# Moving the values of a 64-token window attention behind the scores, two pairs at a time

## The reference, cut to what matters

```python
def _layer(x, wqkv, qs, ksc, wo, lg, lb, w1, b1, w2, b2):
    h = shift_token(x)              # second half of the channels, one token later
    q, k, v = split_heads(h @ wqkv) # 8 heads of 64
    q = l2norm(q) * qs
    k = l2norm(k) * ksc
    q, k = rotary_xpos(q, k)
    # 64-token windows, each sees itself and the window before it:
    sim = einsum('bhwid,bhwjd->bhwij', q * 8, k)  # masked
    attn = softmax(sim)
    o = einsum('bhwij,bhwjd->bhwid', attn, v)
    x = x + o @ wo
    ...                             # token shift, layer norm, gated MLP
```

## Time and profile before

| | |
|---|---|
| median of 3 runs | 2771.79 us |
| the profiled execution | 2765.04 us, its span 2763.1 us |
| PE busy | 2596.0 us, 94% |
| ACT busy | 1839.9 us, 67% |
| DVE busy | 1642.4 us, 59% |
| POOL busy | 1025.6 us, 37% |
| mean granted clock of PE | 0.983 |

### The profile page before, as it was taken

How to read it: one execution, slowest core, us unless ns; L and a number is a source line. 1 busy time by engine, 2 the same in 40 slices (tenths; PEclk the granted TensorE clock), 3 DMA queues, 4 the chain that set the end, 5 groups by cost and what they waited for, 6 DMA issues and landing times.

```text
span 2763.1 us, 61433 instructions
## 1 busy us (share of the span) xinstructions
PE 2596.0 (94%) x23844; PEld 1789.5 (65%) x23844; DVE 1642.4 (59%) x4295; ACT 1839.9 (67%) x4424; POOL 1025.6 (37%) x876
## 2 busy tenths in 40 slices
PE   7999999899999998999999997998998998988998
PEld 4655656449899884788888883554555663553554
DVE  6564747475545548556666666774774236755774
ACT  6676767427676661778787875875785417776775
POOL 2332323213323310545454533552553014542551
PEclk9999999999999998999999999999999999999999
DMA  1010000000000002000000003111210002201210
GB/s 59 1 44 1 13 10 1 4 9 2 2 2 2 2 2 61 21 2 2 2 2 2 2 2 127 47 35 28 54 47 5 25 20 60 49 20 35 50 39 16
DMA packets 35411, 63.13 MB, mean 23 GB/s; under 512 B 11542, under 2 KB 15670, under 8 KB 34102
## 3 DMA queue, kind: packets, MB, share of 16 engines
q1 hardware_dynamic: 35126, 59.21, 7.8%
HBM read 23.62 MB, written 1.15 MB: 9 GB/s over the span
## 4 chain that ended last, share of the span: by engine, by line
PE 76%; DVE 8%; ACT 7%; issue 3%; SPq 3%; POOL 1%; DMA 1%; DVEq 0%; POOLq 0%; ACTq 0%
PE bank L807 65%; PE bank L1036 6%; PE bank L1173 3%; SPq L772 3%; ACT work L1430 1%; ACT work L1323 1%; PE bank L883 1%; DVE work L1619 1%; ACT bank L1299 1%; ACT squared L1301 1%; DMA work<-work 1%; ACT squared L1295 1%; ACT work L1291 1%; POOL work L1993 1%; DVE centered L1550 1%
## 5 line engine op out<-in xcount | busy, mean ns | idle before, releaser
L1749 DVE TENSOR_REDUCE low<-bank 128x1 f32<-128x512 f32 (+22 forms) x512 | 292.9, 573 | 290.6 <-PE bank L807 288.8
L1291 ACT ACTIVATE low<-bank 128x512 f32<-128x512 f32 (+3 forms) x544 | 434.4, 919 | 0.0
L807 PE MATMUL bank<-table_keys,halves 128*128 128x512 f32 (+3 forms) x1536 | 414.9, 378 | 2.6 <-ACT low L1384 2.4
L807 PE MATMUL bank<-work 128*64 128x128 f32 (+6 forms) x4192 | 343.2, 294 | 40.8 <-DVE work L1841 20.4
L807 PEld LDWEIGHTS bank<-work 128*64 128x64 f32 (+4 forms) x4192 | 248.6, 144 | 204.7 <-issue 149.8
L1384 ACT ACTIVATE low<-bank,low 128x512 f32<-128x512 f32 (+23 forms) x384 | 224.9, 586 | 228.4 <-DVE low L1749 223.2
L1944 POOL TENSOR_TENSOR halves<-squared,const 128x512 fp32r<-128x512 f32 x128 | 135.6, 1060 | 502.1 <-PE bank L807 502.1
L1291 ACT ACTIVATE work<-bank 128x512 f32<-128x512 f32 (+4 forms) x389 | 199.8, 539 | 132.9 <-PE bank L807 67.9
L807 PEld LDWEIGHTS bank<-table_keys,halves 128*128 128x128 f32 x1536 | 241.9, 189 | 42.2 <-issue 11.9
L1430 ACT ACTIVATE work<-work 128x192 f32<-128x192 f32 (+1 forms) x512 | 218.7, 431 | 38.5 <-DVE work L1834 38.5
L1993 POOL TENSOR_TENSOR work<-work 128x768 f32<-128x768 f32 x128 | 187.7, 1467 | 136.0 <-DVE work L1845 136.0
(11 more groups left out here) (203 smaller groups left out, 5373.2 us busy)
## 6 DMA issues: line engine op xcount, KB each, us to landing
work<-work SPq DMA_DIRECT2D x512, 64.0 KB, 2.0
slot<-in_wW SPq DMA_DIRECT2D x4, 1605.5 KB, 6.6
slot<-in_wA SPq DMA_DIRECT2D x4, 837.0 KB, 6.1
table_low<-embv_padded SPq DMA_DIRECT2D x2, 1536.0 KB, 6.4
table<-in_dft SPq DMA_DIRECT2D x1, 3072.0 KB, 11.7
slot<-in_wE SPq DMA_DIRECT2D x2, 584.0 KB, 3.8
squared<-in_x SPq DMA_DIRECT2D x4, 256.0 KB, 6.4
shifted<-embv_padded SPq DMA_DIRECT2D x2, 512.0 KB, 8.2
```

The lines of the kernel that those rows point to most:

```text
L807: return pe.matmul(o, l, r, start=start, stop=stop)
L1291: return act.activation(dst, src, ACT.Identity)
L1749: dve.tensor_reduce(out=NBR[:, t.G % 4:t.G % 4 + 1], in_=bank[t.G % 2][:, 0:score_columns(t)], axis=AX.X, op=ALU.max, negate=True).then_in ...
```

## The change

The values step of the loop now does both pairs of one `hp` at once. It stands in every even step from the fifth on, right behind the scores and ahead of the projection, and takes the pairs j - 4 and j - 3; the heads copy follows the exponentials of the same step. `TW` has four buffers. The token shift at the start of a stage goes lane by lane; the clearing of `PW` is moved behind the last lane's shift, and DVE's first reduction of a stage waits for it.

```diff
@@ stage_w, the loop over the steps
                     add("w_scores", c=lane, i=i, hp=hp)
+                if j >= 4 and j % 2 == 0:
+                    lane, i, hp = pairs[j - 4]
+                    held = add("w_values", c=lane, i=i, hp=hp, u=first + j - 4)
                 if r < C * lane_items:
                     rotate(r)
                 if j < len(pairs):
+                    lane, i, hp = pairs[j]
                     add("w_exps", c=lane, i=i, hp=hp)
-                if 2 <= j <= len(pairs) + 1:
-                    lane, i, hp = pairs[j - 2]
-                    if i == 0:
-                        held = add("w_values", c=lane, i=i, hp=hp, u=first + j - 2)
-                    else:
-                        add("w_values_on", c=lane, i=i, hp=hp, u=first + j - 2, tile=held)
-                        add("w_heads", c=lane, hp=hp, tile=held)
+                if j >= 4 and j % 2 == 0:
+                    lane, i, hp = pairs[j - 4]
+                    add("w_heads", c=lane, hp=hp, tile=held)
                 if r < C * lane_items:
                     length(r)
@@ buffers
-        TW = carve(2, 2, T)
+        TW = carve(4, 2, T)
@@ PE
-            def head_values(s, o):
-                pe.wait_ge(sem("w_turned_act"), s.u + 1)
-                pe.wait_ge(sem("w_turned_dve"), s.u + 1)
-                for u in range(2):
-                    i = s.i + u
+            def w_values(s):
+                if s.hp == 0:
+                    pe.wait_ge(sem("w_v_copied"), NT * (s.u // 8 + 1))
+                pe.wait_ge(sem("w_turned_act"), s.u + 2)
+                pe.wait_ge(sem("w_turned_dve"), s.u + 2)
+                o = take(s.k)
+                for i in range(NT):
                     for blk in range(0 if i else 1, 2):
                         for a in range(2):
                             h = 2 * s.hp + a
                             last = mm(o[a * 64:(a + 1) * 64, i * P:(i + 1) * P], VW[:, s.c % 2, i - 1 + blk, h * 64:(h + 1) * 64],
-                                      TW[:, s.u % 2, u, (2 * a + blk) * P:(2 * a + blk + 1) * P],
+                                      TW[:, (s.u + i // 2) % 4, i % 2, (2 * a + blk) * P:(2 * a + blk + 1) * P],
                                       start=(blk == (0 if i else 1)), stop=(blk == 1))
...
+                last.then_inc(tile_full, 1)
@@ ACT, w_heads
-                act.wait_ge(sem("w_valued"), s.n + 1)
-                copy(AW[:, s.hp, :], tile_of(s.tile.k)[:, :]).then_inc(sem("w_heads_copied"), 1)
+                copy(AW[:, s.hp, :], full(s.tile.k)[:, :]).then_inc(sem("w_heads_copied"), 1)
@@ DVE, w_scores
+                if s.c == 0 and s.hp == 0 and s.i == 0:
+                    dve.wait_ge(sem("pad_cleared"), s.n // (DEPTH_W * C * PAIRS * NT // 2) + 1)
@@ POOL, shift
-                if s.c == 0 and s.via == "norm":
-                    for lane in range(C):
-                        source_ready(pool, s, lane)
-                    stage = s.n // (2 * DEPTH_W * C)
-                    pool.memset(PW.rearrange("p a b t -> p (a b) t")[:, :, 0:P], 0.0).then_inc(sem("pad_cleared"), 1)
-                    pool.wait_ge(sem("pad_cleared"), stage + 1)
                 pool.tensor_copy(shifted[0:half, s.c, :], inner[0:half, s.c, :])
                 pool.tensor_copy(shifted[half:P, s.c, 1:T], inner[half:P, s.c, 0:T - 1]).then_inc(sem("shift_done"), 1)
                 pool.wait_ge(sem("shift_done"), s.n + 1)
+                if s.c == C - 1 and s.via == "norm":
+                    stage = s.n // (2 * DEPTH_W * C)
+                    pool.memset(PW.rearrange("p a b t -> p (a b) t")[:, :, 0:P], 0.0).then_inc(sem("pad_cleared"), 1)
+                    pool.wait_ge(sem("pad_cleared"), stage + 1)
```

More of the change, by code:

```diff
@@ L1275, in _ @@
                          w_rotate=w_rotate, w_length=w_length, w_value=w_value, w_scores=w_scores, w_turn=w_turn,
-                         w_values=w_values, w_values_on=w_values_on, w_out=w_out, w_mlp=w_mlp, h_kernels=h_kernels,
+                         w_values=w_values, w_out=w_out, w_mlp=w_mlp, h_kernels=h_kernels,
                          h_project=h_project, h_turn=h_turn, h_forward=h_forward, h_inverse=h_inverse, h_out=h_out)
@@ L1434, in turned_columns @@
                 v, lo = "p (a b t) -> p a b t", 0 if s.i + u else 1
-                return (TW[:, s.n % 2, u].rearrange(v, a=2, b=2)[:, :, lo:2, :], bank_[:, :].rearrange(v, a=2, b=2)[:, :, lo:2, :])
+                return (TW[:, s.n % 4, u].rearrange(v, a=2, b=2)[:, :, lo:2, :], bank_[:, :].rearrange(v, a=2, b=2)[:, :, lo:2, :])
             def w_turn(s):
@@ L1840, in w_turn @@
                 o = full(s.k + 1)
-                dve.tensor_copy(TW[:, s.n % 2, 1], o[:, :]).then_inc(sem("w_turned_dve"), 1)
+                dve.tensor_copy(TW[:, s.n % 4, 1], o[:, :]).then_inc(sem("w_turned_dve"), 1)
             def w_weigh(s):
@@ L1911, in shift @@
                     pool.wait_ge(sem("first_cleared"), 1)
-                if s.c == 0 and s.via == "norm":
-                    for lane in range(C):
-                        source_ready(pool, s, lane)
+                pool.tensor_copy(shifted[0:half, s.c, :], inner[0:half, s.c, :])
+                pool.tensor_copy(shifted[half:P, s.c, 1:T], inner[half:P, s.c, 0:T - 1]).then_inc(sem("shift_done"), 1)
+                pool.wait_ge(sem("shift_done"), s.n + 1)
+                if s.c == C - 1 and s.via == "norm":
                     stage = s.n // (2 * DEPTH_W * C)
@@ L1918, in shift @@
                     pool.wait_ge(sem("pad_cleared"), stage + 1)
-                pool.tensor_copy(shifted[0:half, s.c, :], inner[0:half, s.c, :])
-                pool.tensor_copy(shifted[half:P, s.c, 1:T], inner[half:P, s.c, 0:T - 1]).then_inc(sem("shift_done"), 1)
-                pool.wait_ge(sem("shift_done"), s.n + 1)
             def gate(s):
```

## The result

| | before | after |
|---|---|---|
| median of 4 runs, us | 2773.27 (2771.15 to 2778.8) | 2823.97 (2821.84 to 2826.74) |
| the profiled execution, us | 2765.04, span 2763.1 | 2821.84, span 2819.9 |
| PE busy, us | 2596.0 | 2594.0 |
| ACT busy, us | 1839.9 | 1840.7 |
| mean granted clock of PE | 0.983 | 0.984 |

The changed kernel is slower: ratio 1.0184, 95% interval 1.017 to 1.0197, which is 51 us. 2812 was forecast, with 2783 to 2836 around it. PE and ACT do the same amount of work as before; what is new is waiting.

What follows compares the result with a forecast made beforehand. PE alone was taken to bound the attention loop. Four loops at +12.6 us give +50.4, the shift -10.0, together +40.4 on the median 2771.8: 2812 us, range 2783 to 2836.

Steps and rivals of the forecast that it cites:

- Projection to length 1.81: In each loop step with a projection, nothing lies between it and its length: 1.81 us start to start, range 1.60 to 2.0.
- 28 values in 1.65: Every second step, 28 value matmul records run together behind the scores, taking 1.65 us.
- +1.32: Steps 4 to 23 of a loop: each pair of steps takes 1.32 us more, ten pairs +13.2 a loop.
- ACT on time: In the step with values, ACT's queue takes 4.36 us between squares, PE needs 4.60: ACT is ready 0.2 early.
- Copies' waits, -1.0: First 24 steps of a loop: waits for ACT's copies of turned probabilities shrink, saving 1.0 us, ends 0 and 1.6.
- the -0.3: Steps 2 and 3 of a loop: the values only vanish there, -0.3 us a loop.
- twice 0.4 for the output projection: Output projection waits for the last heads copy: 0.2 to 0.4 us lost, twice a loop, +0.7.
- The last eight steps, 0: Loop steps without a projection: taken as 0 us a loop, between ends -5.0 and +3.8.
- The two halves: Last eight steps: up to 5.0 us of values' waits for DVE's copies won, against doubled values delaying turns, up to 3.8.
- Shift, -10: Start of the two stages: lane-by-lane shift brings ACT's first square 5.0 us earlier, twice, -10.0 us, ends -10 and 0.
- The faster rival: Loop: fewer mode changes and vanished values' waits win, and the length finds its square ready; 2718 us, chance 0.05.
- The rival of the clock: First 24 steps of the loops: PE's short stalls lower its granted clock to 0.96, 21 us more, 2833; chance 0.03.

## Why the prediction was right, point by point

- **Projection to length 1.81:** right. It is 1.81 or 1.82 in steps 4 to 23 of all four loops, taken from the one place in the old trace that had nothing in between the earlier trace rows. The runs with a later length, and with values or a value projection in between, make the idle time go exactly where something lies between.
- **28 values in 1.65:** measured 1.68. Two steps: 10.54 against 9.22, +1.32 as forecast.
- **ACT on time:** right, with 0.49 to spare where 0.2 was reckoned. It becomes the bound only once the wait for the square is removed, which the run with the later length shows.
- **Copies' waits, -1.0:** about -0.8, as what is left over. Ten pairs of steps at 1.32, the -0.3 and twice 0.4 for the output projection (which came as forecast: 0.39 each) make 13.7; measured 12.9.
- **The last eight steps, 0:** this is the term that was mis-sized. It is 2.8 + 0.9 = 3.7 a loop, 15 us in all, at the high end that was named (3.8). The two halves were thought to cancel. The gain did not come, since the wait for the weighing stands right behind those waits for copies and takes their place, as the single values three steps back show. The cost came in full and more: fewer values ahead of the turn uncover POOL's order (add, then weighing), and in three of four loops the wait is followed by a dip of the clock. About half of it, 7 us, goes with single values at the end, and exchanging POOL's add takes back 0.7 to 2.2 a loop by its trace; the two were not run together, so how far they overlap is open. In the old order the same exchange only moves the wait to the next step.
- **Shift, -10:** 4.7 and 5.0 in the trace, 11 us by the run of the shift alone.
- **The sum.** By the runs of single parts the loop costs 60.7 where 50.4 was forecast, and the shift gives 11.0 where 10.0 was. By the trace the loops cost 66.4, and nearly all that is over the forecast is the term of the last eight steps; 12.9 for the first 24 steps stands against 12.6 forecast.

The faster rival had the price of a change between kinds of matmul right. A projection behind split matmuls takes 1.05 before another split group (above, 1748.27 to 1749.32) and 0.96 before a full one (1738.08 to 1739.04), so a change is 0.1. That agrees in kind with the Trainium skill (TensorEngine Tiling (Array Packing), Key Properties), that a change of tiling mode drains the engine. Three changes of 0.1 fewer in two steps stand against two waits of 0.69.

The rival of the clock did not come where it was put: a pause of 0.69 about every 5 us left the granted clock at 1.00 from 1742 to 1840. It came behind single longer waits, at 0.64 for 4.7 us behind the 1.93 of the first loop, and there not in every loop. The Trainium skill (TensorE: Matmul & The Clock Gate, "A second HAM failure mode: psum-queue depth-cycling") tells of a clock that goes back and forth where PE idles for short times between its groups; the loop here does not show that.

## What to carry to other kernels

An operand that goes to another engine and comes back has a fixed price (here 1.8 us for projection, square and length), and the matmuls put in between are what pays for it. So, before independent work is gathered into larger groups, ask which round trip it covered. Read the price from a place in the trace where the cover is missing already, often the first step of a loop. Then look at the steps where the loop runs out: an order on a side engine that was covered can come to the path there.

The version that beats both kernels is the shift alone, 2760.11 (0.9961); the add behind the weighing (2758.67) and the deeper buffers (2760.87) change nothing that can be measured beside it.

## What the runs showed of the hardware that was not expected

- POOL's copies and DVE's norms slow each other. At the stage start the copies at 1679.06, 1680.11 and 1681.10 take 0.98, 0.95 and 1.06, and the norms at 1678.63 and 1679.81 take 0.94 and 0.78; alone they take 0.60 and 0.69. The run with the shift alone shows the same 0.94, 0.98, 0.78, 0.95. The Trainium skill (SBUF — State Buffer, "SBUF: two separate sides") says that DVE, in an operation with two inputs from that memory, and POOL share a pair of ports that the first holds for the whole instruction while the other waits. The rows agree: each of these copies ends 0.47 after the end of the norm that began before it (1680.04 after 1679.57, 1681.06 after 1680.59, 1682.16 after 1681.69), and each of these norms 0.55 after the end of the copy that began before it (1679.57 after 1679.02, 1680.59 after 1680.04). The first lane's shift is 0.37 later for it than two copies of 0.61 would be.
- The clock fell behind single waits of PE of about 2 us, but not behind each. Of the four waits of 1.93 to 2.50 in step 25 of the changed kernel three were followed by some us at the lower level; of the waits of 1.85 in the second step of a loop, one of four in the kernel before and one of four in the changed kernel; of the four waits of 0.87 in step 25 with the add behind the weighing, none. A dip in the second step cost 1.4 us.
